# Where two of four heads get their edge mask in the last attention layer of a four-layer graph network

## The chip, the core and the metric

One NeuronCore of one Trainium2 chip runs the whole network in one launch. The metric is the device time in microseconds (us), lower is better. The engines are PE (TensorE: matrix products), DVE (VectorE), ACT (ScalarE), POOL (GpSimd) and SP (SyncE, which only issues transfers). They run side by side and wait for each other by semaphores.

## What is computed

128 graphs of 128 nodes with 128 features go through four layers, each followed by a residual and a layer norm. The change touches the last one, a masked attention with four heads of 32 columns:

```python
Q = jnp.einsum('bnd,hde->bhne', node_embeddings, Wq)
K = jnp.einsum('bnd,hde->bhne', node_embeddings, Wk)
V = jnp.einsum('bnd,hde->bhne', node_embeddings, Wv)
scores = jnp.einsum('bhne,bhme->bhnm', Q, K) * scale
mask = adjacency_matrices[:, None, :, :] > 0
scores = jnp.where(mask, scores, -jnp.inf)
attn = jax.nn.softmax(scores, axis=-1)
heads = jnp.einsum('bhnm,bhme->bhne', attn, V)
return concat @ Wo.T + bo
...
x = _layernorm(x + _L3_gnn_ref(x, adj, ...), axis=-1)
```

The exponentials of the non-edges must not count, neither in a head's product nor in its denominator. This can be had before the exponential (a large negative number is added to the score) or behind it (the exponential is multiplied by the 0/1 adjacency).

## The kernel before

The last layer is the function `heads`. A step takes `NG` = 4 graphs, side by side in 512 columns, so there are `T` = 32 steps. Each engine has its own program of one order of work, written out by hand in its `step(t, slot, lap)`; an engine runs its instructions strictly in that order, and `need(engine, semaphore, count)` makes it wait. The steps are software-pipelined: in step t, an engine may work for t-2 up to t+3.

PE, in step t: `scores(t)`, `transpose_x(t+2)` (L1619), `keys(t+1)` (L1630, into the bank `KD`), `project(t-1)` (L1677, the output matrix), `queries(t+1)` (L1625), `vals(t+1)` (L1635), `attend(t)` (L1662: 16 products of the heads, into `QO`), `denominators(t)` (L1669: for each head the exponentials times a block of ones, into `KD`). All operands are f32, except those of the mask products. In `scores`, the third and fourth head (h = 2, 3) begin with a product that lays a mask under the scores (L1644, bf16): `far` is the identity times -2^100, and `nota` is 1 - adjacency. The products of queries and keys (L1651) are then added to it.

ACT, in step t: the exponentials of heads 0 and 1 (`exps`, L1448), a copy of the transposed x for t+2 (`evac_xt`, L1432), the exponentials of heads 2 and 3, copies of the queries and values (`evac_q` L1437, `evac_v` L1442), small roots for t-2, and `reciprocals(t)` (L1455, L1458: exp(-ln) of the denominators), which waits for `denominators(t)`.

POOL, in step t: it issues the load of the adjacency for t+2 (`load_adj`, L1400, a ring of four buffers), multiplies the exponentials of heads 0 and 1 by the adjacency, in place (`mask`, L1405), and adds the bias to x (`biased`, L1410, tile `xb`).

DVE, in step t: `divide(t-1)` (L1528, the heads times the reciprocals), `invert(t+1)` (L1522, makes `nota`), `evac_k(t+1)` (L1517, the keys), `finish(t-1)` (L1533, the projected heads plus `xb`), `statistics(t-1)` (L1540), `moments(t-1)` (L1549 to L1555, five tiny operations), `normalize(t+3)` (L1510, the input's norm) and `result(t-2)` (L1562, the output's norm). `pp` holds the exponentials of all heads, in two buffers.

In one step, `end.first` puts thirteen small operations on a flag into DVE's program (L2046 to L2063), behind `result` of step 27.

Of the kernel before, what the change touches and what calls it, by code (L numbers as in the profile page):

```python
# [7 lines left out]
BF16 = mybir.dt.bfloat16  # L8
# [6 lines left out]
N = 128  # L15
D = 128
EPS = 1e-5
NG = 4
# [6 lines left out]
def need(eng, sem, value):  # L25

    if isinstance(value, int) and value <= 0:
        return
    eng.wait_ge(sem, value)
# [1095 lines left out]
def relational(nc, sb, sem, pb, k, yres, stats, const, before, after, adjbad, layer1, block, later, adj_mgn):  # L1125
# [95 lines left out]
    @block.vector  # L1221
    def _(dve):
        def normalize(n, slot):
            if known(n):
                dve.wait_ge(before.done, 1)
            for g in range(NG // 2):
                at = n * NG + g
                ins = nc.vector.tensor_scalar(xr[:, slot, g, :], yres[:, bass.ds(at, 1), :].rearrange("p o d -> p (o d)"),
                                              before.mean[:, bass.ds(at, 1)], before.rstd[:, bass.ds(at, 1)], ALU.subtract, ALU.mult)
            ins.then_inc(s["ln"], 1)  # L1230

        def values(n, slot):
            need(dve, s["tanh"], n + 1)
            need(dve, s["o"], n - 1)
            h = HG[slot % 2].rearrange("p (g k d) -> p g k d", g=NG, k=2)[:, :, 0, :]
            nc.vector.scalar_tensor_tensor(vv[:, slot % 2], th[:, slot % 2], 1.0, h, ALU.add, ALU.mult).then_inc(s["v"], 1)

        def finish(n, slot):
            need(dve, s["o"], n + 1)
            nc.vector.scalar_tensor_tensor(yres[:, bass.ds(n * NG, NG), :], O[slot % 2].rearrange("p (g d) -> p g d", g=NG), 0.0,  # L1240
                                           xr[:, slot, :, :], ALU.max, ALU.add).then_inc(s["y_out"], 1)

        def statistics(n, slot):
            need(dve, s["y_out"], n + 1)
            for g in range(NG):
                at = n * NG + g
                ins = nc.vector.bn_stats(stats[:, bass.ds(at, 1), :].rearrange("p o d -> p (o d)"),
                                         yres[:, bass.ds(at, 1), :].rearrange("p o d -> p (o d)"))
            ins.then_inc(s["stats"], 1)

        block.normalize = normalize

        def step(t, slot, lap):
            if known(t) and t == T - 6:
                dve.wait_ge(s["stats"], RING + 4)
                after.variance(dve, 0)
            if known(t) and t == T - 4:
                after.refine(dve, 0)
            if not known(t) or t >= 1:
                finish(t - 1, (slot - 1) % R8)  # L1260
            if not known(t) or t + 3 < T:
                normalize(t + 3, (slot + 3) % R8)
            if not known(t) or t + 1 < T:
                values(t + 1, (slot + 1) % R8)
            if known(t) and t >= T - 3:
                later.normalize(t - T + 3, t - T + 3)
            if known(t) and t == T - 1:
                later.evac_k(0, 0)
                later.invert(0, 0, 0)
            if not known(t) or t >= 1:  # L1270
                statistics(t - 1, (slot - 1) % R8)
            if known(t) and t == 0:
                layer1.last()
                const.excess(dve)
            if known(t) and t == 4:
                before.refine(dve, 1)
            if known(t) and t == 8:
                later.set_tiles()

        def rest():  # L1280
            values(0, 0)
            steps(dve, step, 26, R8, 10)

        def last():
            finish(T - 1, (T - 1) % R8)
            statistics(T - 1, (T - 1) % R8)

        def variance():
            dve.wait_ge(s["stats"], T)
            after.variance(dve, 1)  # L1290

        block.last, block.variance = last, variance
        return rest
# [57 lines left out]
def heads(nc, sb, sem, pb, k, yres, stats, const, before, rsum, layer2, block, end, adjt, out_ngd):  # L1351
# [11 lines left out]
    xr = sb("x3", [N, RING, NG, D], F32)  # L1363
    xt = sb("xt3", [D, 2, NG * N], F32)
    adj = sb("adj3", [N, RING, NG * N], BF16)
    nota = sb("nota3", [N, 2, NG * N], BF16)
    far = sb("far3", [N, N], BF16)
    onesh = sb("onesh3", [N, E], F32)
    rise = sb("rise3", [N, 1], F32)
    xb = sb("xb3", [N, 2, NG, D], F32)  # L1370
# [7 lines left out]
    lden = sb("lden3", [D, NG * N], F32)  # L1378
    rec = sb("rec3", [D, 2, NG * N], F32)
    on = sb("on3", [D, 2, NG * N], F32)  # L1380
    s = {n: sem(f"l3_{n}") for n in ("set ln xt_tr xt q qt kk kt v va rise pm nota xb link sq half var lvar root out s p o den log rec on "
                                     "w y_out").split()}
    adj_in = [sem(f"l3_adj_in{r}") for r in range(RING)]

# [10 lines left out]
    @block.gpsimd  # L1395
    def _(pool):
        def load_adj(n, slot):
            need(pool, s["nota"], n - 3)
            need(pool, s["pm"], 2 * (n - 3))
            pool.dma_start(adj[:, slot, :].rearrange("p (g n) -> p g n", g=NG),  # L1400
                           adjt[:, bass.ds(n * NG, NG), :]).then_inc(adj_in[slot], 16)

        def mask(n, h, slot):
            need(pool, s["p"], H * n + h + 1)
            nc.gpsimd.tensor_tensor(pp[:, slot % 2, h], pp[:, slot % 2, h], adj[:, slot], ALU.mult).then_inc(s["pm"], 1)  # L1405

        def biased(n, slot):
            need(pool, s["ln"], n + 1)
            need(pool, s["y_out"], n - 1)
            nc.gpsimd.tensor_tensor(xb[:, slot % 2], xr[:, slot], k["bo"][:, :].rearrange("p (o d) -> p o d", o=1).to_broadcast([N, NG, D]),  # L1410
                                    ALU.add).then_inc(s["xb"], 1)

        def step(t, slot, lap):
            if not known(t) or t + 2 < T:
                load_adj(t + 2, (slot + 2) % RING)
            mask(t, 0, slot)
            mask(t, 1, slot)
            biased(t, slot)

        def rest():  # L1420
            load_adj(0, 0)
            load_adj(1, 1)
            steps(pool, step, 26)

        return rest
# [76 lines left out]
    def _(dve):  # L1502
# [13 lines left out]
            need(dve, s["s"], n - 1)  # L1516
            nc.vector.tensor_copy(kt[:, slot % 2, :], KD[:, :]).then_inc(s["kt"], 1)  # L1517

        def invert(n, slot, lap):
            need(dve, adj_in[slot], 16 * (lap + 1))  # L1520
            need(dve, s["s"], n - 1)
            nc.vector.tensor_scalar(nota[:, slot % 2, :], adj[:, slot, :], -1.0, 1.0, ALU.mult, ALU.add).then_inc(s["nota"], 1)  # L1522

        def divide(n, slot):
            need(dve, s["o"], n + 1)
# [37 lines left out]
            ins.then_inc(s["out"], 1)  # L1563

        def set_tiles():
            nc.vector.tensor_scalar(far[:, :], k["ident"][:, :], -2.0 ** 100, None, ALU.mult)
            nc.vector.memset(eps[:, :], EPS)
            nc.vector.memset(onesh[:, :], 1.0).then_inc(s["set"], 1)

        block.set_tiles, block.normalize, block.evac_k, block.invert = set_tiles, normalize, evac_k, invert  # L1570

        def step(t, slot, lap):
            a1, a3, c0 = (slot + 1) % RING, (slot + 3) % RING, (slot - 1) % RING
# [3 lines left out]
            if inc:  # L1577
                divide(t - 1, c0)
            if in1:
                invert(t + 1, a1, lap + (slot + 1) // RING)  # L1580
            if in1:
                evac_k(t + 1, a1)
            if inc:
                finish(t - 1, c0)
                statistics(t - 1, c0)
                moments(t - 1, c0)
            if in3:
# [25 lines left out]
    def _(pe):  # L1613
# [23 lines left out]
            ins.then_inc(s["v"], 1)  # L1637

        def scores(n, slot):
            need(pe, s["nota"], n + 1)  # L1640
            need(pe, s["p"], H * (n - 1) + 2)
            for h in range(2, H):
                need(pe, s["p"], H * (n - 1) + h + 1)
                nc.tensor.matmul(S[h][:, :], far[:, :], nota[:, slot % 2, :], start=True, stop=False, skip_group_check=True)  # L1644
            need(pe, s["qt"], n + 1)
            need(pe, s["kt"], n + 1)
            for g in range(NG):
                c = slice(g * N, (g + 1) * N)
                for h in range(H):
                    r = slice(h * E, (h + 1) * E)  # L1650
                    ins = nc.tensor.matmul(S[h][:, c], kt[r, slot % 2, c], qt[r, slot % 2, c], start=(h < 2), stop=(h < 2 or g == NG - 1),  # L1651
                                           skip_group_check=True)
            ins.then_inc(s["s"], 1)

        def attend(n, slot):
            need(pe, s["p"], H * (n + 1))
            need(pe, s["pm"], 2 * (n + 1))
            need(pe, s["va"], n + 1)
            need(pe, s["qt"], min(n + 2, T) if known(n) else n + 2)
            for g in range(NG):  # L1660
# [3 lines left out]
            ins.then_inc(s["o"], 1)  # L1664

        def denominators(n, slot):
            need(pe, s["kt"], min(n + 2, T) if known(n) else n + 2)
            for h in range(H):
                ins = nc.tensor.matmul(KD[h * E:(h + 1) * E, :], onesh[:, :], pp[:, slot % 2, h, :], start=True, stop=True,  # L1669
                                       skip_group_check=True)  # L1670
            ins.then_inc(s["den"], 1)
# [15 lines left out]
        def step(t, slot, lap):  # L1687
# [11 lines left out]
            if in1:  # L1699
                queries(t + 1, a1)  # L1700
                vals(t + 1, a1)
            attend(t, slot)
            denominators(t, slot)

        def rest():
            vals(0, 0)
# [539 lines left out]
```

## Time and profile before

| | us |
|---|---|
| median of 3 runs (746.05 to 750.06) | 747.95 |
| the profiled execution, its own time | 748.71 |
| its span (first to last instruction) | 744.6 |
| PE busy, share of the span | 92% |
| DVE busy | 83% |
| ACT busy | 75% |
| POOL busy | 53% |

The last layer takes the time from 484.3 to about 740 us. Its 32 steps are all alike but for the first two, the one with the flag's operations, and the last. "Busy" is the time in which an engine had an instruction of its own under way, a stall inside an instruction included. An instruction's duration runs from its start to its end; on one engine the next may start some hundredths before that end.

### The profile page before, as it was taken

How to read it: one execution, taken by the hardware profiler on the slowest of the kernel's cores; microseconds unless marked ns; L12 is line 12 of the kernel's file. 1: busy time of each engine (PE TensorE's matmuls, PEld its weight loads, DVE VectorE, ACT ScalarE, POOL GpSimd, SP SyncE). 2: the span in 40 equal slices, each digit the busy share in tenths (PEclk: the TensorE clock that was granted, in tenths of full speed). 3: DMA queues.
4: the chain of work that ended last, by engine and by line, in shares of the span. 5: the costliest groups of instructions: out<-in, count | busy, mean ns of one | idle time of the engine just before them, and what ended most of it. 6: DMA issues, size and time to landing. Idle time of an engine off the chain costs nothing.

```text
span 744.6 us, 25853 instructions
## 1 busy us (share of the span) xinstructions
PE 686.7 (92%) x8484; PEld 507.2 (68%) x8484; DVE 620.2 (83%) x1782; ACT 559.8 (75%) x1266; POOL 394.8 (53%) x591
## 2 busy tenths in 40 slices
PE   5999999999988889999779999899999999999892
PEld 4677777777765667677568999766676666676561
DVE  2589999999898699999988888877778787878865
ACT  3576777777756899999678999777777778787572
POOL 4478778877886344444351112355464645555431
PEclk9799999999999999999999999999999999999997
DMA  7234434443320122232114332312222222222201
GB/s 219 84 120 125 113 105 122 119 120 101 113 69 15 28 36 36 35 35 35 15 46 121 88 88 72 65 16 44 59 47 49 56 49 56 47 58 44 50 35 53
DMA packets 34908, 51.97 MB, mean 70 GB/s; under 512 B 4388, under 2 KB 14376, under 8 KB 34856
## 3 DMA queue, kind: packets, MB, share of 16 engines
q1 hardware_dynamic: 20600, 34.36, 14.9%
q0 software_dynamic: 13968, 16.82, 13.9%
q8 instruction: 29, 0.48, 0.3%
q14 instruction: 23, 0.19, 0.1%
q10 hardware_dynamic: 288, 0.13, 0.1%
HBM read 51.32 MB, written 8.39 MB: 80 GB/s over the span
## 4 chain that ended last, share of the span: by engine, by line
PE 71%; DVE 18%; issue 5%; ACT 3%; DVEq 1%; POOL 1%; DMA 1%; SPq 0%; ACTq 0%; POOLq 0%
PE banks L751 9%; PE banks L1310 6%; PE banks L738 5%; PE banks L707 5%; PE banks L759 5%; PE banks L1651 4%; PE banks L1677 4%; PE banks L1662 4%; DVE pp L979 4%; PE banks L1625 4%; PE banks L1635 4%; PE banks L1630 3%; PE banks L1669 3%; PE banks L728 3%; PE banks L1318 3%
## 5 line engine op out<-in xcount | busy, mean ns | idle before, releaser
L626 DVE SCALAR_TENSOR_TENSOR pp<-banks,floor,adj 128x1024 f32<-128x1024 f32 x128 | 159.5, 1266 | 6.4 <-PE banks L738 5.4
L1405 POOL TENSOR_TENSOR pp<-pp,adj 128x512 f32<-128x512 f32 x64 | 73.4, 1162 | 129.1 <-ACT pp L1448 129.1
L1448 ACT ACTIVATE pp<-banks,nobound 128x512 f32<-128x512 f32 x128 | 81.5, 696 | 3.6 <-PE banks L1651 1.9
L751 PE MATMUL banks<-pp,yv 128*17 128x128 f32 x2048 | 82.8, 280 | 0.7 <-issue 0.5
L864 POOL TENSOR_TENSOR yres<-oo,x 128x512 f32 (+1 forms) x32 | 40.5, 1264 | 73.9 <-DVE oo L997 73.9
L533 ACT COPY rows<-banks 128x640 bf16<-128x640 bf16 x64 | 44.3, 692 | 42.5 <-PE banks L728 42.5
L1310 PE MATMUL banks<-w2b,xt 128*128 128x256 f32 x256 | 60.6, 380 | 3.0 <-ACT xt L1182 3.0
L751 PEld LDWEIGHTS banks<-pp,yv 128*17 128x17 f32 x2048 | 45.6, 98 | 15.6 <-issue 2.0
L738 PE MATMUL banks<-rows 32*128 32x128 bf16 x1024 | 51.5, 221 | 5.1 <-DVE pp L626 5.0
L897 ACT ACTIVATE x<-yres,nmr,rstd 128x128 f32 (+1 forms) x128 | 55.7, 490 | 0.0
L452 POOL TENSOR_TENSOR oo<-turned,rall 128x512 f32<-128x512 f32 x32 | 33.8, 1057 | 37.1 <-DVE rall L632 37.1
L1455 ACT ACTIVATE lden<-banks,rise 128x512 f32<-128x512 f32 x32 | 22.0, 687 | 40.3 <-PE banks L1669 40.3
L1310 PEld LDWEIGHTS banks<-w2b,xt 128*128 128x128 f32 x256 | 46.1, 190 | 8.2 <-issue 3.3
L1677 PEld LDWEIGHTS banks<-w3ot,on 128*128 128x128 f32 x256 | 34.4, 197 | 22.8 <-DVE on L1528 16.5
L538 ACT COPY ot<-banks 128x512 f32<-128x512 f32 x64 | 37.5, 586 | 15.5 <-PE banks L751 15.5
L707 PE MATMUL banks<-w0e,xt 128*128 128x144 f32 x256 | 47.2, 313 | 1.9 <-DVE banks L645 1.5
L1149 POOL DMA_DIRECT2D adj<-in_adj x32 | 17.3, 543 | 56.8 <-ACT sq L1194 54.2
L1082 PE MATMUL banks<-yv,pp 128*128 128x129 f32 x256 | 36.0, 283 | 10.2 <-DVE oo L990 10.2
L738 PEld LDWEIGHTS banks<-rows 32*128 32x128 bf16 x1024 | 29.2, 94 | 22.7 <-issue 11.2
L1635 PEld LDWEIGHTS banks<-w3v,xt 128*128 128x128 f32 x256 | 33.7, 192 | 15.4 <-issue 14.9
L459 POOL TENSOR_TENSOR yres<-oo,x 128x512 f32 (+1 forms) x32 | 40.7, 1272 | 6.3 <-POOL oo L452 5.7
L759 PE MATMUL banks<-ident,ot 128*128 128x128 f32 x256 | 42.8, 290 | 0.5 <-ACT turned L543 0.5
(214 smaller groups left out, 1921.6 us busy)
## 6 DMA issues: line engine op xcount, KB each, us to landing
xt<-in_xt SPq DMA_DIRECT2D x32, 256.0 KB, 2.8
adj<-in_adjt SPq DMA_DIRECT2D x32, 256.0 KB, 2.7
x<-in_x SPq DMA_DIRECT2D x32, 256.0 KB, 2.7
adj<-in_adjt POOLq DMA_DIRECT2D x64, 128.0 KB, 3.0
adj<-in_adj POOLq DMA_DIRECT2D x32, 256.0 KB, 3.0
out_ngd<-yres SPq DMA_DIRECT2D x32, 256.0 KB, 2.0
ident<-in_ident ACTq DMA_DIRECT2D x1, 64.0 KB, 2.2
w0t<-in_w0t SPq DMA_DIRECT2D x1, 64.0 KB, 2.0
```

The source lines that it names most:

```text
L533: nc.scalar.copy(rows[:, slot % 2, a, :], R[:, 0:5 * N]).then_inc(s["rw"], 1)
L626: nc.vector.scalar_tensor_tensor(pp[:, g], S[g % 2][:, :].rearrange("p (h n) -> p h n", n=N), floor[:, slot:slot + 1], adj[:, slot, g:g + ...
L707: ins = nc.tensor.matmul(at[:, g, :], xt[:, slot, 2 * half + g, :], k["w0e"][:, :], start=True, stop=True, skip_group_check=True)
L738: ins = nc.tensor.matmul(S[g % 2][:, c:c + N], rows[at, slot % 2, g // 2, (1 + q) * N:(2 + q) * N], rows[at, slot % 2, g // 2, 0:N], start ...
L751: ins = nc.tensor.matmul(O[32 * h:32 * h + w, c:c + N], yv[:, slot % 2, g * H + 4 * half + h, :], pp[:, g, 4 * half + h, :], start=True, s ...
L759: ins = nc.tensor.transpose(X[:, c * N:(c + 1) * N], ot[:, a, c * N:(c + 1) * N], k["ident"][:, :])
L897: ins = nc.scalar.activation(xr[:, slot, g, :], flat(at), ACT.Identity, bias=before.nmr[:, bass.ds(at, 1)], scale=before.rstd[:, bass.ds(a ...
L1310: ins = nc.tensor.matmul(out, xt[:, slot % 2, g, :], k["w2b"][:, :], start=True, stop=True, skip_group_check=True)
L1405: nc.gpsimd.tensor_tensor(pp[:, slot % 2, h], pp[:, slot % 2, h], adj[:, slot], ALU.mult).then_inc(s["pm"], 1)
L1448: nc.scalar.activation(pp[:, slot % 2, h], S[h][:, :], ACT.Exp, bias=k["nobound"][:, :], scale=SCALE).then_inc(s["p"], 1)
L1635: ins = nc.tensor.matmul(XV[:, g * D:(g + 1) * D], xt[:, slot % 2, g * N:(g + 1) * N], k["w3v"][:, :], start=True, stop=True)
L1677: ins = nc.tensor.matmul(WF[:, g * D:(g + 1) * D], on[:, slot % 2, g * N:(g + 1) * N], k["w3ot"][:, :], start=True, stop=True)
```

## The change

The third and fourth head are masked like the first two, behind their exponentials, but by DVE instead of POOL. DVE's `invert` and the products with `far` go, with their tiles and the semaphore `nota`; DVE gets `mask(t, 2)` behind `evac_k(t+1)` and `mask(t, 3)` behind `finish(t-1)`, and counts them on a new semaphore `vm`. On PE, `denominators(t)` comes in front of `attend(t)`, and is now what waits for all exponentials and masks. `load_adj` waits for DVE's masks where it waited for `nota`. POOL now waits for the adjacency itself, in front of its first mask.

```diff
         def load_adj(n, slot):
-            need(pool, s["nota"], n - 3)
             need(pool, s["pm"], 2 * (n - 3))
+            need(pool, s["vm"], 2 * (n - 3))
...
-        def mask(n, h, slot):
+        def mask(n, h, slot, lap):
+            if h == 0:
+                need(pool, adj_in[slot], 16 * (lap + 1))
             need(pool, s["p"], H * n + h + 1)
...
-        def invert(n, slot, lap):
-            need(dve, adj_in[slot], 16 * (lap + 1))
-            need(dve, s["s"], n - 1)
-            nc.vector.tensor_scalar(nota[:, slot % 2, :], adj[:, slot, :], -1.0, 1.0, ALU.mult, ALU.add).then_inc(s["nota"], 1)
+        def mask(n, h, slot, lap):
+            if h == 2:
+                need(dve, adj_in[slot], 16 * (lap + 1))
+            need(dve, s["p"], H * n + h + 1)
+            nc.vector.tensor_tensor(pp[:, slot % 2, h], pp[:, slot % 2, h], adj[:, slot], ALU.mult).then_inc(s["vm"], 1)
...
             if in1:
-                invert(t + 1, a1, lap + (slot + 1) // RING)
-            if in1:
                 evac_k(t + 1, a1)
+            mask(t, 2, slot, lap)
             if inc:
                 finish(t - 1, c0)
+            mask(t, 3, slot, lap)
+            if inc:
                 statistics(t - 1, c0)
                 moments(t - 1, c0)
...
         def scores(n, slot):
-            need(pe, s["nota"], n + 1)
-            need(pe, s["p"], H * (n - 1) + 2)
-            for h in range(2, H):
-                need(pe, s["p"], H * (n - 1) + h + 1)
-                nc.tensor.matmul(S[h][:, :], far[:, :], nota[:, slot % 2, :], start=True, stop=False, skip_group_check=True)
+            need(pe, s["p"], H * n)
...
         def attend(n, slot):
-            need(pe, s["p"], H * (n + 1))
-            need(pe, s["pm"], 2 * (n + 1))
             need(pe, s["va"], n + 1)
...
         def denominators(n, slot):
+            need(pe, s["p"], H * (n + 1))
+            need(pe, s["pm"], 2 * (n + 1))
+            need(pe, s["vm"], 2 * (n + 1))
             need(pe, s["kt"], min(n + 2, T) if known(n) else n + 2)
...
-            attend(t, slot)
             denominators(t, slot)
+            attend(t, slot)
```

DVE's program of step 26 before the change, where PE's products wait for `on` (from `divide`), `nota` and `kt` (the keys):

```order
L1528 TENSOR_TENSOR on_101<-banks,rec_100 128x512
L1522 TENSOR_SCALAR nota_88<-adj_87 128x512
L1517 COPY kt_84<-banks 128x512
L1533 TENSOR_TENSOR yres<-banks,xb_92 128x512
L1540 BN_STATS stats<-yres 128x6 x4
L1549 TENSOR_TENSOR apart_95<-stats 128x4
L1550 TENSOR_TENSOR both_94<-stats 128x8
```

And with the change (the same step):

```order
L1528 TENSOR_TENSOR on_99<-banks,rec_98 128x512
L1516 COPY kt_84<-banks 128x512
L1522 TENSOR_TENSOR pp_82<-pp_82,adj_87 128x512
L1533 TENSOR_TENSOR yres<-banks,xb_90 128x512
L1522 TENSOR_TENSOR pp_82<-pp_82,adj_87 128x512
L1540 BN_STATS stats<-yres 128x6 x4
L1549 TENSOR_TENSOR apart_93<-stats 128x4
L1550 TENSOR_TENSOR both_92<-stats 128x8
```

One operation of 128x512 is gone, and two others, on `pp`, stand to both sides of the one that writes `yres`; L1522 is now the line of DVE's mask.

PE's program of one step before the change, from the mask products to the denominators (`onesh` is the block of ones):

```order
L1644 MATMUL banks<-nota_88,far_89 128x512 x2
L1651 MATMUL banks<-qt_83,kt_84 128x128 x16
L1619 MATMUL banks<-ident,x_85 128x128 x4
L1630 MATMUL banks<-xt_86,w3k 128x512
L1677 MATMUL banks<-w3ot,on_101 128x128 x4
L1625 MATMUL banks<-xt_86,w3q 128x512
L1635 MATMUL banks<-w3v,xt_86 128x128 x4
L1662 MATMUL banks<-pp_82,va_93 32x128 x16
L1669 MATMUL banks<-pp_82,onesh_90 32x512 x4
```

And with the change:

```order
L1647 MATMUL banks<-qt_83,kt_84 128x128 x16
L1619 MATMUL banks<-ident,x_85 128x128 x4
L1630 MATMUL banks<-xt_86,w3k 128x512
L1674 MATMUL banks<-w3ot,on_99 128x128 x4
L1625 MATMUL banks<-xt_86,w3q 128x512
L1635 MATMUL banks<-w3v,xt_86 128x128 x4
L1666 MATMUL banks<-pp_82,onesh_88 32x512 x4
L1656 MATMUL banks<-pp_82,va_91 32x128 x16
```

The two products with `far` are gone, and the four with `onesh` have moved in front of the sixteen with `va`.

## Rows read from the trace of the kernel before

**Rows 1.** Busy time, by stretch: us; then per engine PE, PEld, DVE, ACT, POOL; granted clock

```profile
484.30:697.10 212.80, 212.32 (x2741) 143.23 (x2744) 167.28 (x581) 163.07 (x332) 114.22 (x112) 1.00 0.23 49
...
700.00:707.00 7.00, 3.86 (x14) 2.83 (x15) 5.62 (x14) 1.28 (x3) 3.02 (x4) 0.76 0.15 19
```

**Rows 2.** The chain that ended last, 642 to 650 us: start, us, what

```profile
642.42 0.86 PE banks L1669 x8
643.28 0.54 PE banks L1644 x2
643.82 1.10 PE banks L1651 x32
644.92 0.59 PE banks L1619 x4
645.51 0.86 PE banks L1630 x2
646.37 0.89 PE banks L1677 x8
647.26 0.86 PE banks L1625 x2
648.12 0.89 PE banks L1635 x8
649.01 1.01 PE banks L1662 x32
```

**Rows 3.** Timeline of one step: start, us, engine, line, operation [idle before, releaser]

```profile
643.75 1.17 PE L1651 MATMUL banks<-qt,kt 32*128 32x128 f32 x32
...
644.99 1.27 ACT L1448 ACTIVATE pp<-banks,nobound 128x512 f32<-128x512 f32 x2
...
645.76 2.31 POOL L1405 TENSOR_TENSOR pp<-pp,adj 128x512 f32<-128x512 f32 x2 [3.51 <-ACT pp L1448]
...
646.40 0.69 DVE L1517 COPY kt<-banks 128x512 f32<-128x512 f32 x1 [0.46 <-PE banks L1630]
646.61 1.29 ACT L1448 ACTIVATE pp<-banks,nobound 128x512 f32<-128x512 f32 x2
...
647.42 0.69 DVE L1533 TENSOR_TENSOR yres<-banks,xb 128x512 f32 x1 [0.33 <-PE banks L1677]
...
648.04 1.26 POOL L1410 TENSOR_TENSOR xb<-x,bo 128x512 f32<-128x512 f32 x1
...
651.35 1.17 PE L1651 MATMUL banks<-qt,kt 32*128 32x128 f32 x32
```

**Rows 4.** Groups of DVE instructions on 512 columns: count | busy us, mean ns | idle before

```profile
L997 DVE SCALAR_TENSOR_TENSOR oo<-ee,oo 128x512 f32<-128x512 f32 x32 | 21.7, 677 | 1.6 <-ACT ee L919 1.6
...
L1522 DVE TENSOR_SCALAR nota<-adj 128x512 bf16<-128x512 bf16 x32 | 9.1, 283 | 0.0
```

**Rows 5.** Timeline, DVE and POOL at the last layer's start and at the flag's operations

```profile
487.53 1.15 POOL L1405 TENSOR_TENSOR pp<-pp,adj 128x512 f32<-128x512 f32 x1
487.59 1.18 DVE L1510 TENSOR_SCALAR x<-yres,mean,rstd 128x128 f32<-128x128 f32 x1
488.65 1.26 POOL L1410 TENSOR_TENSOR xb<-x,bo 128x512 f32<-128x512 f32 x1
488.69 1.30 DVE L1510 TENSOR_SCALAR x<-yres,mean,rstd 128x128 f32<-128x128 f32 x1
...
490.18 0.34 DVE L1510 TENSOR_SCALAR x<-yres,mean,rstd 128x128 f32<-128x128 f32 x1
...
700.07 0.15 DVE L2059 TENSOR_TENSOR flag_col<-flag_col 128x1 f32<-128x1 f32 x1
...
701.21 1.25 POOL L1410 TENSOR_TENSOR xb<-x,bo 128x512 f32<-128x512 f32 x1
701.30 1.18 DVE L2063 TENSOR_TENSOR flag_col<-flag_col 128x1 f32<-128x1 f32 x1
```

**Rows 6.** Transfers by group: size, median us from issue to landing

```profile
adj<-in_adjt POOLq DMA_DIRECT2D x64, 128.0 KB, 3.0
```

More of the change, by code:

```diff
@@ L1268, in step @@
                 later.evac_k(0, 0)
-                later.invert(0, 0, 0)
             if not known(t) or t >= 1:
@@ L1365, in heads @@
     adj = sb("adj3", [N, RING, NG * N], BF16)
-    nota = sb("nota3", [N, 2, NG * N], BF16)
-    far = sb("far3", [N, N], BF16)
     onesh = sb("onesh3", [N, E], F32)
@@ L1380, in heads @@
     on = sb("on3", [D, 2, NG * N], F32)
-    s = {n: sem(f"l3_{n}") for n in ("set ln xt_tr xt q qt kk kt v va rise pm nota xb link sq half var lvar root out s p o den log rec on "
+    s = {n: sem(f"l3_{n}") for n in ("vm set ln xt_tr xt q qt kk kt v va rise pm xb link sq half var lvar root out s p o den log rec on "
                                      "w y_out").split()}
@@ L1415, in step @@
                 load_adj(t + 2, (slot + 2) % RING)
-            mask(t, 0, slot)
-            mask(t, 1, slot)
+            mask(t, 0, slot, lap)
+            mask(t, 1, slot, lap)
             biased(t, slot)
@@ L1565, in set_tiles @@
         def set_tiles():
-            nc.vector.tensor_scalar(far[:, :], k["ident"][:, :], -2.0 ** 100, None, ALU.mult)
             nc.vector.memset(eps[:, :], EPS)
             nc.vector.memset(onesh[:, :], 1.0).then_inc(s["set"], 1)
-        block.set_tiles, block.normalize, block.evac_k, block.invert = set_tiles, normalize, evac_k, invert
+        block.set_tiles, block.normalize, block.evac_k = set_tiles, normalize, evac_k
         def step(t, slot, lap):
@@ L1650, in scores @@
                     r = slice(h * E, (h + 1) * E)
-                    ins = nc.tensor.matmul(S[h][:, c], kt[r, slot % 2, c], qt[r, slot % 2, c], start=(h < 2), stop=(h < 2 or g == NG - 1),
+                    ins = nc.tensor.matmul(S[h][:, c], kt[r, slot % 2, c], qt[r, slot % 2, c], start=True, stop=True,
                                            skip_group_check=True)
@@ L1701, in step @@
                 vals(t + 1, a1)
+            denominators(t, slot)
             attend(t, slot)
-            denominators(t, slot)
         def rest():
```

## The prediction

> **What bounds the kernel now.** I read first the busy time by stretch. Over 28 whole steps of the last layer (484.3 to 697.1 us) PE is busy for 212.32 of 212.80 us, at the full granted clock, DVE for 167.28, ACT for 163.07, POOL for 114.22 [rows 1]. So PE sets the pace there. The chain of waits says the same: it runs through PE alone, and its nine pieces are one step, 0.86 + 0.54 + 1.10 + 0.59 + 0.86 + 0.89 + 0.86 + 0.89 + 1.01 = 7.60 us [rows 2]. The timeline agrees: the scores' products start at 643.75 and again at 651.35 [rows 3]. What is taken from PE's list is gained, until another engine or a chain of waits needs longer than the list that is left. A difference under 0.5% could not be told from no change with this kernel.
>
> **What goes from PE.** Both mask products of a step: 0.54 us [rows 2]. PE's list is then 7.06 us, and 32 steps would bring 17.3 us. The other products keep their sizes, and the swap of two neighbours costs nothing in itself: the denominators need the keys evacuated from their bank, and that copy ends at 647.09, over 2 us before they could start [rows 3].
>
> **What goes from DVE and comes to it.** `nota` goes: 0.28 us [rows 4]. Two multiplications of 128x512 come, with f32 data and a bf16 mask, both from SBUF. No row has just this. The nearest is the f32 operation on two SBUF tiles of that shape, 0.68 us, and I take it; from below the bf16 operation with 0.28 bounds it, though that moves half the bytes [rows 4]; from above 0.69, an operation of that shape from a PSUM bank [rows 3]. DVE's busy time per step was 167.28/28 = 5.97; it becomes 5.97 - 0.28 + 2 x 0.68 = 7.05 us. By this sum alone DVE and PE are level, and DVE has a few short waits for its own results besides. The filling of `far`, once, lies outside the loop: nothing.
>
> **The new chain of waits.** More counts than busy time. Before, only PE's first products on `pp` waited for ACT's exponentials and POOL's two masks, and these were early. Now the denominators wait for four masks, and two of them are at places in DVE's program. From the scores' start at 643.75, as offsets [rows 3]: ACT's exponentials 0 and 1 start at 1.24, 2 and 3 at 2.86. Half of that pair's 1.29, and the tail of the first, makes exponential 2 done at about 3.5. POOL's two masks run from 2.01 to 4.32, with `xb` right behind (4.29). DVE's copy of the keys ends at 3.34. So DVE would ask for mask 2 at about 3.55, in the middle of POOL's second mask.
>
> There DVE is held. Where one operation of DVE meets one of POOL, both on SBUF, DVE's takes as long as POOL's does: the flag's operation on a single column took 1.18 us beside a POOL operation that ended 0.02 before it, where its neighbour took 0.15; the norm's, of 128 columns, took 1.18 and 1.30 instead of 0.34 [rows 5]. In that stretch the first ran in between two operations of POOL, and the second, which came 0.04 behind the start of POOL's next, waited for nearly all of that. So it is one at a time, each for its whole operation, and whoever asks first goes first. The overlap at a change from POOL to DVE: the first of them ended at 488.77, so it ran from 488.43, 0.25 before POOL's recorded end at 488.68; for the flag's it is 702.48 - 0.15 = 702.33, 0.13 before 702.46 [rows 5]. From DVE to POOL, `xb` could be recorded from 488.65 on, 0.12 before DVE's end, and took its usual 1.26 [rows 3, 5].
>
> So in line: POOL's second mask until 4.32; mask 2, 0.68: 5.00; `xb`, 1.26: 6.26 (DVE's `finish` runs beside it, having one input from PSUM, as the copy of the keys does beside POOL's masks now); mask 3, 0.68: 6.94. Less 0.25 twice and 0.12 once: 6.32. Then PE's denominators (0.86) and heads (1.01) come before the next scores: 6.32 + 1.87 = 8.19 us per step, against 7.60. PE is then idle for 8.19 - 7.06 = 1.1 us of each step, in front of the denominators.
>
> Bounds of this term: with overlaps of 0.13, 8.43; with masks of 0.60 (a little under the nearest row), 8.03; with no overlap at all, 8.81. Whether `xb` too is held by mask 2 no row of before shows (DVE never was first there); if it were not, `xb` would end at 5.55, mask 3 would go on from 5.3 to 6.0, and the step would be 7.87. I take the held one, since the second of the norm's operations shows a single holder.
>
> The Trainium skill (SBUF — State Buffer, "Who interferes with whom") states it both ways: a VectorE instruction with two SBUF inputs and a GpSimd instruction that reads SBUF exclude each other, and the second to come is blocked for the whole of the first. By that rule the 7.87 falls away and 8.19 stays; that DVE waits, the trace shows (1.18 us for a single column), that POOL waits no row here shows.
>
> **The rest.** The loads of the adjacency now wait for DVE's masks of two steps earlier; they land 3.0 us after issue [rows 6] and are asked for two steps ahead, some 15 us, so they cost nothing even with DVE's masks late. POOL waits for the adjacency in front of its first mask, which DVE did in its place: nothing. The reciprocals start earlier relative to the heads, by the heads' 1.01, but DVE's `result` block keeps DVE from using it: nothing. Attending later by one group is inside the 1.87. With PE idle for over a microsecond a step the clock could fall; in the flag's stretch, with PE busy for 3.86 of 7.00 us, it was 0.76 [rows 1]. A gap of 1.1 us is far shorter than the single long one there: I charge nothing, and leave it to the upper end.
>
> **The sum.** 8.19 - 7.60 = 0.59 us for each of 32 steps, +18.9 us; first and last steps are charged like the others. From the profiled execution's 748.71 that is 767.6; this execution lies 0.76 above the median of the runs, so against the median 766.8. I say 767. With steps from 7.87 to 8.6 it is 757 to 780.
>
> **The rivals.**
> 1. The masks meet no hold: f32 with bf16 behaves otherwise than the flag's f32, or `xb` and masks dodge each other. Then mask 2 goes from 3.55, `finish` and mask 3 follow at distances of 0.61 (DVE's operations start a little before the last one's end), and mask 3 ends at 3.55 + 0.61 + 0.61 + 0.68 = 5.45; the step is 5.45 + 1.87 = 7.32, a little more with DVE's own waits at a load of 7.05. That is 0.15 to 0.28 less than now: 739 to 744 us, faster. For it: no row has a bf16 operand in such a meeting. Against: the multiplication reads two SBUF tiles like those that were held.
> 2. PE's list is the bound: 7.06 us per step, 731 us. It needs no hold and masks much shorter than 0.68; at 0.28 the chain would be 6.5. This is the change doing all that its sum on PE promises.
> 3. POOL keeps its turn at both changes. POOL's three operations stand back to back, and if the next one always beats a waiting DVE, mask 2 goes only after `xb`: 2.01 + 2.31 + 1.22 = 5.54; with mask 2, `finish` and mask 3 (0.61 + 0.61 + 0.68), less 0.25, 7.19, and the step is 9.06, 795 us. Against it stands the norm's first operation, which came in between. A fall of the clock would end up in this region too.
>
> **How the numbers follow.** Held, by turns (7.87 to 8.6): 0.63. Rival 1: 0.12. Rival 2: 0.05. Rival 3, or a mix of both orders: 0.20. The likeliest case's own range is 757 to 780. From 742 to 790 leaves out rival 2, half of rival 1 and about half of rival 3, 0.2 in all. Faster by over 0.5%: rival 2 and most of rival 1, 0.14. Within 0.5%: the end of rival 1, and a hold made up for by shorter masks, 0.08. Slower: 0.78.
>
> **What would show it.** Right: the steps last 8.0 to 8.4 us; PE shows an idle time of about 1 us in front of the denominators, ended by DVE's `pp`; DVE's masks have two durations far over 0.7, about 1.1 for the first of a step (it waits for POOL's second mask) and 1.0 for the second (it waits for `xb`); POOL's `xb` is longer than 1.26. Wrong: both masks at 0.7 (rival 1 or 2, and PE without gaps would mean rival 2); a first mask of over 2 us (rival 3); a clock under 1.00 in mid-layer. I would be wrong in the sign if DVE's masks came at moments at which POOL is at rest.

## The result, and the profile after

The changed kernel takes 778.4 us (777.46 to 782.0, 6 runs) against 747.88 us for the one before: ratio 1.0414, 95% interval 1.0391 to 1.0437. It is 30.5 us slower. The forecast was 767 us in a range of 742 to 790, with a chance of 0.78 for slower. All times and ratios below come from fast runs; each ratio is against runs of the kernel before that were taken together with it, whose median moved between 747.09 and 750.22 us, so variants are best compared by their ratios. The profiled execution took 777.53 us, its span is 773.0 us against 744.6.

The timeline of one whole step in mid-layer is the view that tells most. Columns: start, us, engine, line, operation; in brackets the idle time before, and what ended it. L1647 are the scores' products, L1522 is VectorE's mask, L1409 is GpSimd's `xb`.

```profile
660.70 1.18 PE L1647 MATMUL banks<-qt,kt 32*128 32x128 f32 x32
...
662.72 2.27 POOL L1404 TENSOR_TENSOR pp<-pp,adj 128x512 f32<-128x512 f32 x2 [3.99 <-ACT pp L1447]
...
663.35 0.69 DVE L1516 COPY kt<-banks 128x512 f32<-128x512 f32 x1
663.56 1.29 ACT L1447 ACTIVATE pp<-banks,nobound 128x512 f32<-128x512 f32 x2
...
664.37 1.17 DVE L1522 TENSOR_TENSOR pp<-pp,adj 128x512 f32<-128x512 f32 x1 [0.32 <-ACT pp L1447]
...
664.95 1.71 POOL L1409 TENSOR_TENSOR xb<-x,bo 128x512 f32<-128x512 f32 x1
...
665.46 0.68 DVE L1533 TENSOR_TENSOR yres<-banks,xb 128x512 f32 x1
...
666.06 1.16 DVE L1522 TENSOR_TENSOR pp<-pp,adj 128x512 f32<-128x512 f32 x1
...
667.32 1.06 PE L1666 MATMUL banks<-pp,onesh 128*32 128x512 f32 x8 [1.12 <-issue]
...
669.18 1.18 PE L1647 MATMUL banks<-qt,kt 32*128 32x128 f32 x32
```

This step lasts 669.18 - 660.70 = 8.48 us, where it lasted 7.60 [rows 3]; 32 times 0.88 is 28.2 us, and the profiled execution has 28.8 more. (Every fourth step is a little longer, 8.56 to 8.58 us; the mean of the 22 steps from 498.94 to 686.25 us is 8.51.) TensorE stands still for 1.12 us in front of the denominators. Both masks take 1.16 to 1.17 us, `xb` takes 1.71 instead of 1.26 [rows 3], and each of the three ends shortly behind the one of the other engine: GpSimd's second mask at 664.99, VectorE's first at 665.54, `xb` at 666.66, VectorE's second at 667.22. The operation between the masks (L1533, one input from PSUM) runs beside `xb` and takes 0.68.

The chain of waits, the same stretch: start, us, what.

```profile
657.71 1.12 issue
658.83 1.06 PE banks L1666 x8
659.89 0.88 PE banks L1656 x32
660.77 1.10 PE banks L1647 x32
661.87 0.59 PE banks L1619 x4
662.46 0.86 PE banks L1630 x2
663.32 1.12 PE banks L1674 x8
664.44 0.86 PE banks L1625 x2
665.30 0.89 PE banks L1635 x8
666.19 1.12 issue
```

In place of the 0.54 us for the mask products [rows 2] there is a gap of 1.12 us, called "issue" since the view names no releaser for it. The timeline shows what ends it: the denominators start at 667.32, 0.10 us behind the end of VectorE's second mask. Over the whole layer the profile puts 7 of these waits, 13.4 us in all, down to VectorE's masks by name. The project products (L1674) take 1.12 instead of 0.89, since `divide` comes a little late; that lies in front of the gap and costs nothing.

Busy time by stretch (us, then PE, PEld, DVE, ACT, POOL, granted clock), and the groups of the two engines from 500 to 680 us:

```profile
484.30:697.10 212.80, 182.46 (x2392) 125.67 (x2390) 191.63 (x543) 145.86 (x298) 112.17 (x101) 1.00 0.20 43
...
724.00:734.00 10.00, 6.87 (x53) 5.12 (x57) 8.87 (x26) 2.80 (x7) 2.77 (x3) 0.66 0.12 15
```

```profile
L1522 DVE TENSOR_TENSOR pp<-pp,adj 128x512 f32<-128x512 f32 x42 | 49.9, 1189 | 5.4 <-ACT pp L1447 5.4
...
L1404 POOL TENSOR_TENSOR pp<-pp,adj 128x512 f32<-128x512 f32 x43 | 48.8, 1149 | 88.4 <-ACT pp L1447 88.4
L1409 POOL TENSOR_TENSOR xb<-x,bo 128x512 f32<-128x512 f32 x21 | 36.0, 1715 | 0.0
```

TensorE's busy share in the layer fell from all of it [rows 1] to 182.46 of 212.80. Its clock stayed at 1.00 in these steps, so the gaps did not cost that. In this layer it is lower only in the flag's stretch, where TensorE idles long in both kernels (0.66 here, 0.76 before [rows 1]), and in the last microseconds, from 755 us on. All 42 of VectorE's masks are long (1.15 to 1.25 us), all 21 of `xb` too (1.71 to 1.72).

### The profile page after: what moved, and what is told of

Its sections match the earlier page's. It is cut to its first block, busy times and chain, and to the rows that moved or that the text cites. A ratio compares the mean times of both kernels' runs of the same rounds, so it can differ in the third digit from the quotient of the medians.

```text
span 773.0 us, 25761 instructions
## 1 busy us (share of the span) xinstructions
PE 680.0 (88%) x8420; PEld 507.9 (66%) x8420; DVE 672.0 (87%) x1813; ACT 559.6 (72%) x1266; POOL 408.4 (53%) x591
## 3 DMA queue, kind: packets, MB, share of 16 engines
q0 software_dynamic: 13968, 16.82, 13.4%
## 4 chain that ended last, share of the span: by engine, by line
PE 65%; DVE 18%; issue 9%; ACT 4%; DVEq 1%; POOL 1%; DMA 1%; SPq 0%; ACTq 0%; POOLq 0%
PE banks L751 9%; PE banks L1309 6%; PE banks L738 5%; PE banks L707 5%; PE banks L759 4%; PE banks L1647 4%; PE banks L1666 4%; PE banks L1674 4%; PE banks L1656 4%; DVE pp L979 3%; PE banks L728 3%; PE banks L1635 3%; PE banks L1625 3%; PE banks L1630 3%; PE banks L1317 3%
## 5 line engine op out<-in xcount | busy, mean ns | idle before, releaser
L1522 DVE TENSOR_TENSOR pp<-pp,adj 128x512 f32<-128x512 f32 x64 | 75.0, 1173 | 10.2 <-ACT pp L1447 10.2
L864 POOL TENSOR_TENSOR yres<-oo,x 128x512 f32 (+1 forms) x32 | 40.4, 1264 | 75.3 <-DVE oo L997 75.3
L1666 PE MATMUL banks<-pp,onesh 128*32 128x512 f32 x256 | 35.0, 615 | 40.1 <-issue 26.7
L1309 PE MATMUL banks<-w2b,xt 128*128 128x256 f32 x256 | 62.2, 387 | 3.0 <-ACT xt L1182 3.0
L1409 POOL TENSOR_TENSOR xb<-x,bo 128x512 f32<-128x512 f32 x32 | 54.4, 1700 | 0.0
L1674 PEld LDWEIGHTS banks<-w3ot,on 128*128 128x128 f32 x256 | 33.0, 200 | 28.4 <-DVE on L1528 22.3
```

The source lines that it names most:

```text
L1309: ins = nc.tensor.matmul(out, xt[:, slot % 2, g, :], k["w2b"][:, :], start=True, stop=True, skip_group_check=True)
L1522: nc.vector.tensor_tensor(pp[:, slot % 2, h], pp[:, slot % 2, h], adj[:, slot], ALU.mult).then_inc(s["vm"], 1)
L1674: ins = nc.tensor.matmul(WF[:, g * D:(g + 1) * D], on[:, slot % 2, g * N:(g + 1) * N], k["w3ot"][:, :], start=True, stop=True)
```

## The experiments

The theory: VectorE and GpSimd hold each other off while both read SBUF, so GpSimd's second mask, mask 2, `xb` and mask 3 stand in one line, and this line, with the denominators, the heads' products and the next scores behind it, sets the step. (A held operation shows no idle time in front of it: its own recorded duration is longer.) The rivals: VectorE's load of about 7 us per step does it, with any kind of operand; the swap of denominators and heads does it.

### 1. The same masks, read from PSUM (e_psum)

```diff
-            nc.scalar.activation(pp[:, slot % 2, h], S[h][:, :], ACT.Exp, bias=k["nobound"][:, :],
+            nc.scalar.activation(pp[:, slot % 2, h] if h < 2 else S[h][:, :], S[h][:, :], ACT.Exp, bias=k["nobound"][:, :],
...
-            nc.vector.tensor_tensor(pp[:, slot % 2, h], pp[:, slot % 2, h], adj[:, slot], ALU.mult).then_inc(s["vm"], 1)
+            nc.vector.tensor_tensor(pp[:, slot % 2, h], S[h][:, :], adj[:, slot], ALU.mult).then_inc(s["vm"], 1)
```

> The changed kernel, but ACT writes the exponentials of heads 2 and 3 in place into their PSUM banks, and VectorE's masks read them there and write pp in SBUF: the same number and shape of operations in the same places, each with one SBUF input instead of two. Theory of the hold (VectorE and GpSimd exclude each other while both read SBUF, so that GpSimd's second mask, mask 2, xb, mask 3 run one behind the other): masks at 0.69 us each without long ones, xb back at 1.26, a step of 7.3 to 7.55 us, 739 to 746 us in all. Rival of the load (VectorE's two more operations and their place behind the exponentials would cost this with any source): 8.3 to 8.5 us per step, 772 to 778 us.

Measured: 745.67 us, ratio 0.998 (0.9958 to 1.0002). Groups, 500 to 680 us:

```profile
L1522 DVE TENSOR_TENSOR pp<-banks,adj 128x512 f32<-128x512 f32 x48 | 32.9, 686 | 5.6 <-ACT banks L1447 5.6
...
L1404 POOL TENSOR_TENSOR pp<-pp,adj 128x512 f32<-128x512 f32 x48 | 54.5, 1148 | 82.7 <-ACT pp L1447 82.7
L1409 POOL TENSOR_TENSOR xb<-x,bo 128x512 f32<-128x512 f32 x24 | 30.4, 1267 | 0.0
```

And from its timeline, GpSimd's masks of two steps, with VectorE's first mask of each:

```profile
598.89 2.27 POOL L1404 TENSOR_TENSOR pp<-pp,adj 128x512 f32<-128x512 f32 x2 [3.37 <-ACT pp L1447]
...
600.44 0.69 DVE L1522 TENSOR_TENSOR pp<-banks,adj 128x512 f32<-128x512 f32 x1 [0.23 <-ACT banks L1447]
...
606.32 2.27 POOL L1404 TENSOR_TENSOR pp<-pp,adj 128x512 f32<-128x512 f32 x2 [3.37 <-ACT pp L1447]
...
607.88 0.69 DVE L1522 TENSOR_TENSOR pp<-banks,adj 128x512 f32<-128x512 f32 x1 [0.23 <-ACT banks L1447]
```

The masks are at 0.69 and `xb` is at 1.27; the mask starts at 600.44 beside GpSimd's second one, and does not wait. This step is 606.32 - 598.89 = 7.43 us; the mean of 23 steps is 7.48. Same operations, same count, same places, same waits; one input of each from PSUM, and the 30 us are gone. The rival of the load falls. Nor is it that both engines read the same tile: they both read `adj` here without a hold, and `xb`, which reads neither `pp` nor `adj`, is held in the changed kernel.

### 2. Without `xb` (e_noxb)

```diff
-            biased(t, slot)
...
-            need(dve, s["xb"], n - 3)
+            need(dve, s["y_out"], n - 3)
...
-            need(dve, s["xb"], n + 1)
...
-                                    xb[:, slot % 2], ALU.add).then_inc(s["y_out"], 1)
+                                    xr[:, slot], ALU.add).then_inc(s["y_out"], 1)
```

> The changed kernel without GpSimd's addition of the bias (xb); VectorE's finish adds x itself, so the output lacks the bias. Theory of the hold: mask 2 still waits for GpSimd's second mask (about 1.17 us), mask 3 is free of it (0.68 us), a step of about 8.0 us (0.46 us less than 8.48), 760 to 764 us. Rival of the load: nothing on VectorE or TensorE has become less, so 8.4 to 8.5 us per step, 776 to 779 us.

Measured: 762.83 us, ratio 1.0217 (1.0185 to 1.0248). Timeline of one step (line numbers are one or two lower here):

```profile
605.35 1.23 DVE L1521 TENSOR_TENSOR pp<-pp,adj 128x512 f32<-128x512 f32 x1 [0.25 <-ACT pp L1446]
...
607.11 0.68 DVE L1521 TENSOR_TENSOR pp<-pp,adj 128x512 f32<-128x512 f32 x1
...
607.88 1.06 PE L1664 MATMUL banks<-pp,onesh 128*32 128x512 f32 x8 [0.64 <-issue]
```

The first mask still waits for GpSimd's second one, the second is free: 0.68 us. So a mask from two SBUF tiles costs 0.68 by itself, the nearest row of before was right, and without `xb` about half of the loss is gone, as the theory had it.

### 3. One mask at a time from PSUM (e_psum_2, e_psum_3)

The edit of the first experiment with `h == 2`, or `h == 3`, in place of heads 2 and 3 together.

> The changed kernel with only head 2's exponentials left in PSUM and masked from there; head 3 is masked out of SBUF as in the changed kernel. Theory of the hold, as a queue for one port: mask 2 takes 0.69 us and is not held, xb starts on time and is back at 1.26, mask 3 asks in its midst and is held until it ends (about 1.2 us), a step of about 8.07 us, 763 to 767 us. Rival (only GpSimd's masks hold VectorE, and mask 2's hold is the whole cost): 7.4 us per step, 745 us.

> The changed kernel with only head 3 in PSUM. Theory of the hold: mask 2 is held by GpSimd's second mask (1.17 us) and holds xb (1.7 us), mask 3 takes 0.69 us beside xb; a step of about 8.0 us, 761 to 765 us, like the run without xb. Rival (the hold of mask 3 alone is the whole cost): 7.4 us per step, 745 us.

Measured: 764.55 us, ratio 1.0206 (1.016 to 1.0252), and 761.87 us, ratio 1.0179 (1.0127 to 1.0231). Timelines of one step, first of e_psum_2:

```profile
604.94 0.69 DVE L1522 TENSOR_TENSOR pp<-banks,adj 128x512 f32<-128x512 f32 x1 [0.23 <-ACT banks L1447]
605.62 1.26 POOL L1409 TENSOR_TENSOR xb<-x,bo 128x512 f32<-128x512 f32 x1
606.15 1.29 DVE L1522 TENSOR_TENSOR pp<-pp,adj 128x512 f32<-128x512 f32 x1
```

Then of e_psum_3:

```profile
604.79 1.24 DVE L1522 TENSOR_TENSOR pp<-pp,adj 128x512 f32<-128x512 f32 x1 [0.26 <-ACT pp L1447]
605.44 1.71 POOL L1409 TENSOR_TENSOR xb<-x,bo 128x512 f32<-128x512 f32 x1
606.55 0.67 DVE L1522 TENSOR_TENSOR pp<-banks,adj 128x512 f32<-128x512 f32 x1
```

In the first, mask 2 asks for nothing, so `xb` starts on time and takes 1.26; mask 3 meets it and waits. In the second, mask 2 waits for GpSimd and `xb` for mask 2, 1.71 again. The long `xb` comes with a mask 2 out of SBUF and goes with it: GpSimd is held by VectorE as VectorE is by GpSimd. Each mask taken out of the line brings some 15 us of the 30.

### 4. The order of heads and denominators (e_attfirst, e_before_swap)

First the changed kernel with the old order on TensorE, the waits moved along; then the kernel before with the new order.

```diff
-            denominators(t, slot)
             attend(t, slot)
+            denominators(t, slot)
```

> The changed kernel with the heads' products in front of the denominators again, the wait for all masks moved with them. Theory of the hold: the masks come as late as before, and now the reciprocals, divide and the projection start later by the 1.01 us of the heads' products, while VectorE has no slack: 8.6 to 9.0 us per step, 782 to 793 us. Rival (the swap itself cost the 30 us, for instance because the denominators then wait for the keys' copy): about 748 us or less.

> The kernel before with the denominators in front of the heads' products, nothing else. Theory of the hold: TensorE stays busy without gaps, 7.60 us per step, 747 to 749 us. Rival (the swap costs): over 755 us.

Measured: 791.31 us, ratio 1.0599 (1.0568 to 1.0631), and 747.82 us, ratio 0.9993 (0.9968 to 1.0017). Of the first, the waits from 500 to 680 us (us in all, times, longest):

```profile
PE banks L1659 <- DVE pp L1522: 29.4, 20, 1.5
...
DVE pp L1522 <- ACT pp L1447: 12.5, 20, 0.7
```

The swap does no harm where it stands alone, and with late masks it saves some 13 us: with the old order TensorE waits up to 1.5 us for the masks instead of 1.12. The timeline of e_attfirst shows why:

```profile
606.62 1.17 PE L1647 MATMUL banks<-qt,kt 32*128 32x128 f32 x32
...
607.55 0.72 ACT L1457 ACTIVATE rec<-lden,excess 128x512 f32<-128x512 f32 x1
...
608.27 1.25 ACT L1447 ACTIVATE pp<-banks,nobound 128x512 f32<-128x512 f32 x2
```

The reciprocals come later by the heads' products, and ScalarE starts the next exponentials only behind them, 1.65 us after the scores' start instead of 1.24 (661.94 - 660.70) in the changed kernel. The masks come later by about as much, and a step takes 8.88 us instead of 8.51. So the rival of the swap falls, and the swap is a part of this change that helped.

### 5. Without VectorE's masks (e_nomask)

`mask(t, 2)`, `mask(t, 3)` and the waits for `vm` are taken out, nothing else. The kernel leaves out the masking of heads 2 and 3.

> The changed kernel without VectorE's two masks: heads 2 and 3 attend to all nodes, which leaves their masking out. Theory of the hold (what TensorE gained is real and was given back through the masks alone): TensorE's list of 7.06 us sets the step, 729 to 733 us, half a millisecond of nothing else. Rival (something else of the change, the order of the products or the new waits, keeps the step long): over 745 us.

(The words on half a millisecond in it carry no meaning.) Measured: 731.19 us, ratio 0.9748 (0.971 to 0.9787). The chain of waits, one step:

```profile
600.20 0.89 PE banks L1670 x8
...
607.26 0.89 PE banks L1670 x8
```

From project to project 7.06 us, and TensorE is busy for all of the 180 us from 500 to 680. What the change takes off TensorE is worth its full 0.54 us per step, 17 us (the ratio says 19; the other 1.5 us were not traced); the masks took that and 30 us more.

### 6. Looking for a version that beats both (e_psum_order, e_psum_split, e_pool3)

Three variants of the PSUM version. In e_psum_order mask 3 stands directly behind mask 2, in front of `finish`. In e_psum_split each head's denominator waits for its own mask:

```diff
             for h in range(H):
+                need(pe, s["pm"] if h < 2 else s["vm"], 2 * n + h % 2 + 1)
```

In e_pool3 GpSimd masks heads 0 to 2, VectorE only head 3, out of PSUM, and the denominators come in the order 0, 1, 3, 2, each behind its own mask.

> The PSUM version with mask 3 directly behind mask 2, in front of finish. By the plain chain (mask 3 is ready 0.6 us after mask 2) the denominators could start 0.6 us earlier, and TensorE's or VectorE's list (7.06 to 7.1 us) would set the step: 731 to 735 us. Theory of the hold, in its second form: VectorE, which has no slack, then does its output norm (tensor_scalar on SBUF) while GpSimd masks, and each such operation may be held for a GpSimd operation, as the norm's were at the layer's start: 7.4 to 7.9 us per step, 742 to 758 us, with output-norm operations far over 0.34 us.

> The PSUM version in which each head's denominator waits for its own mask only. If the wait of the denominators for mask 3 ends the step (0.65 us of products could come in front of it): 7.1 to 7.4 us per step, 733 to 743 us. If VectorE's list sets the step, no change against the PSUM version's 7.43 us, 745 us.

> GpSimd masks heads 0, 1 and 2 in SBUF, VectorE only head 3, out of PSUM, and each head's denominator waits for its own mask, head 2 last. GpSimd has 5.9 of some 7.3 us to do, VectorE 6.4. Theory of the hold: VectorE's mask is not held (0.69 us), no long one left but small ones of the moments, 7.1 to 7.4 us per step, 733 to 742 us. Rival of the load, turned to GpSimd (its third mask ends 5.45 us behind the scores' start and holds up the denominators): 7.4 us or more, over 742 us.

Measured: e_psum_order 766.38 us, ratio 1.0234 (1.019 to 1.0279); e_psum_split 744.27 us, ratio 0.9914 (0.9884 to 0.9944); e_pool3 744.13 us, ratio 0.993 (0.9904 to 0.9957).

The first is the instructive miss of the plain chain, that is, of the sum in which nothing is held. Its timeline shows two kinds of steps by turns (from 562 us on the output norm, L1562, `tensor_scalar` on SBUF, takes 1.11 us in every second step and 1.95 to 3.00 in those between; the steps last 7.1 to 7.2 and 8.9 to 11.5 us); one of each:

```profile
603.74 1.11 DVE L1562 TENSOR_SCALAR yres<-yres,both,inv  x4
...
605.05 2.27 POOL L1404 TENSOR_TENSOR pp<-pp,adj 128x512 f32<-128x512 f32 x2 [4.64 <-ACT pp L1447]
...
611.64 3.00 DVE L1562 TENSOR_SCALAR yres<-yres,both,inv  x4
...
612.24 2.32 POOL L1404 TENSOR_TENSOR pp<-pp,adj 128x512 f32<-128x512 f32 x2 [3.13 <-ACT pp L1447]
...
615.29 1.01 PE L1673 MATMUL banks<-w3ot,on 128*128 128x128 f32 x5 [2.00 <-DVE on L1528]
```

In the short step the scores, and with them GpSimd's masks, come earlier relative to VectorE, which then does its output norm in their midst: 3.00 us instead of 1.11, `divide` behind it is late, and TensorE waits 2.00 us. In the next step the norm is over before GpSimd's masks start, and it is short again.

The longest steps hold a second cost, that of TensorE's clock. The two rows are the long step shown, and another long one (us, then PE, PEld, DVE, ACT, POOL, granted clock):

```profile
610.22:621.67 11.45, 9.06 (x101) 6.09 (x97) 10.68 (x32) 5.96 (x12) 4.10 (x4) 0.85 0.22 44
645.83:655.62 9.79, 7.40 (x101) 4.99 (x97) 9.09 (x27) 5.84 (x12) 4.10 (x4) 1.00 0.24 51
```

TensorE idles for 2.39 us in both. In the first, its clock falls behind the 2.00 us of waiting: the granted clock is 0.63 from 615.3 to 619.9 us, so that it ran for most of them at 1.2 GHz, the lower of its two levels, and the same products take 1.66 us more. Two steps between 500 and 700 us are of this kind, 3.3 us in all; why the clock fell in these and not in the other long ones is open. The second form of the theory is borne out in kind, but the time lies above its upper end (766 against 758 us), and 3.3 us of that are the clock's.

The other two are small gains: the whole interval of their ratio lies below 1. They beat both kernels, by 0.7 to 0.9% against the one before. Neither met its expectation: e_psum_split's 744.27 us lies between its two cases (733 to 743, and 745), and e_pool3's 744.13 is above the 733 to 742 of the theory and where its rival had put it (over 742). But the cause in e_pool3 is not the rival's: no instruction of TensorE is recorded as waiting for a mask there. In e_pool3 the weight loads of the project products wait for `divide`, 17.0 us in 180 [first row], and VectorE's `finish` in turn waits for the project products [second row]. The products themselves leave TensorE hardly idle (busy for 178.08 of 180 us), but the project ones take 1.16 us instead of 0.89. In e_psum_split these weight loads wait for `divide` as well, 15.0 us in 180. That this loop through `divide` sets the step of about 7.4 us is read from the waits, and no run tests it.

```profile
PEld banks L1672 <- DVE on L1529: 17.0, 19, 0.9
DVE yres L1534 <- PE banks L1672: 16.1, 25, 0.8
```

Getting to the 7.06 us of TensorE's list was not achieved.

## Why the prediction was right, and where its size was off

**TensorE's list**: right, 7.06 us, shown by e_nomask.

**The size of a mask**: 0.68 by the nearest row, 0.68 measured where it is free (e_noxb).

**The hold**: right in kind and in order. VectorE's mask 2 waits for GpSimd's second mask, `xb` for mask 2, mask 3 for `xb`. That GpSimd is held too was the assumption no row of before carried (7.87 us per step without it); 1.71 us for `xb`, and 1.26 where mask 2 reads PSUM, carry it now. The Trainium skill (SBUF — State Buffer, "Who interferes with whom") had it as a rule that a VectorE instruction with two SBUF inputs contends with a GpSimd instruction that reads SBUF. The runs agree with it: beside GpSimd's operations the masks take 1.16 to 1.29 us in the steps shown with both inputs in SBUF and 0.69 with one in PSUM. That one SBUF input is not safe for every operation, the output norm shows (experiment 6).

**The sum**: 8.19 us per step forecast, 8.48 measured in the step shown. The time, 778.4 us, lies near the upper end of the 757 to 780 that the likeliest case had; the signs asked for steps of 8.0 to 8.4 us and a second mask of 1.0 us, which took 1.16. The term that was mis-sized is the overlap at the changes from GpSimd to VectorE. I took 0.25 us twice, from the norm's row; with 0.68 us of its own, mask 2 ran from 664.86, 0.13 before GpSimd's recorded end at 664.99, and mask 3 from 666.54, 0.12 before 666.66. That is 0.25 us more. The flag's row had 0.13, and my bound with it (8.43) was nearly right. The other part is the way from mask 3's end to the denominators' start, 667.22 to 667.32, 0.10 us, which I had not charged. Smaller ones (GpSimd's masks end 0.03 earlier, `xb` overlaps 0.14 instead of 0.12, the products take 1.86) take 0.06 off. 0.25 + 0.10 - 0.06 = 0.29, and 32 times that is 9.3 of the 11.4 us that 767 was short. About 1 us more is that the mean step is 8.51 and not 8.48; the rest was not traced further.

**VectorE's load**: put too high. The sum gave 7.05 us per step; in e_psum, with the same operations and none held, VectorE is busy for 161.31 of 180 us, 6.70 of a step of 7.48. The forecast did not rest on it.

**Costs taken as nothing**: the loads of the adjacency and POOL's wait for the adjacency show no wait, and the clock stayed at 1.00 in spite of 1.12 us of idle time in each step. The swap costs nothing, but that the earlier reciprocals are worth nothing was wrong: the forecast took the exponentials' start at 1.24 us from the kernel before, and with late masks it is the swap that keeps it there (1.65 in e_attfirst, some 13 us in all).

**The rivals**: no hold (739 to 744 us) is what e_psum runs into when it is made so, at 7.43 us per step, 0.11 above the 7.32 worked out, since there too the denominators start 0.10 behind the last mask, and 745.67 us. TensorE's list as the bound (731) is what e_nomask reaches, without the two masks. POOL's keeping its turn (795) did not occur: VectorE came in between two operations of GpSimd each time, as the norm's first operation had.

## What to carry to other kernels

Before work is moved to VectorE, look at where its inputs are and at what GpSimd does at that moment: here a VectorE operation with two SBUF inputs and a GpSimd one did not run side by side (1.17 us instead of 0.68 for a mask, 1.71 instead of 1.26 for `xb`), and in a chain through both engines their durations added, less some 0.13 us per change. Leave one input in PSUM where there is a choice: here ScalarE wrote its exponentials in place for the same price, and some 32 us went. And where an engine has little slack (VectorE, busy for 6.70 of 7.48 us in e_psum), an order that looks shorter on paper can come out longer, when it slides under the other engine's operations, as in e_psum_order.

## What the runs showed that I had not expected

- Steps of two lengths by turns in a program whose steps are all alike (e_psum_order). That the hold alone makes them alternate is read from the timeline; no run tests it.
- The hold goes for `tensor_scalar` with one f32 SBUF input as well, at its full weight (e_psum_order): four operations took 3.00 us instead of 1.11 beside GpSimd's masks. The rows of before had shown this at the layer's start; I had used them for the masks and not asked where else it would strike.
- ScalarE's exponentials take the same whether they go to SBUF or back into their PSUM bank: a pair takes 1.26 us both ways (e_psum):

```profile
599.73 1.26 ACT L1447 ACTIVATE banks<-banks,nobound 128x512 f32<-128x512 f32 x2
...
605.54 1.26 ACT L1447 ACTIVATE pp<-banks,nobound 128x512 f32<-128x512 f32 x2 [0.37 <-PE banks L1647]
```
